# A decoder layer's scan stage: two products for each tile of the small projection, and the attention stage's key stacks loaded by halves of the heads

## The reference

```
x = x + scan(layernorm(x));  x = x + attention(layernorm(x), ctx, ctx);  x = x + experts(layernorm(x))

scan:      xz = x @ W_in.T;  x_proj, z = split(xz)            # 1024 columns each
           x_conv = silu(conv_b + causal convolution over 4 steps)
           x_dbl = x_conv @ W_xproj.T                         # 33 columns: B (16), C (16), dt (1)
           dt = clip(softplus(x_dbl[..., -1]), 0.001, 0.1)
           h = clip(exp(dt*A)*h + clip(dt*B)*x_t, -100, 100);  y_t = h . C
           out = (y*silu(z) + x_conv*D) @ W_out.T
attention: 16 heads of 32; scores = q k^T / sqrt(32); softmax; @ v; @ Wo.T + bo
experts:   top 2 of 8 experts with a capacity; silu(x W1 + b1) W2 + b2
```

## Time and profile before

| | us |
|---|---|
| median of 3 runs | 2587.34 (2586.89 to 2590.86) |
| profiled execution | 2590.91 |
| its span | 2589.3 |
| PE busy in the span | 2419.5 (93%) |
| VectorE busy | 1493.9 (58%) |
| ScalarE busy | 1198.0 (46%) |
| POOL busy | 647.5 (25%) |
| mean granted TensorE clock | 0.968 of full speed |

### The profile page before, as it was taken

How to read it: one execution, slowest core, us unless ns; L and a number is a source line. 1 busy time by engine, 2 the same in 40 slices (tenths; PEclk the granted TensorE clock), 3 DMA queues, 4 the chain that set the end, 5 groups by cost and what they waited for, 6 DMA issues and landing times. The chain is left out here.

```text
span 2589.3 us, 47800 instructions
## 1 busy us (share of the span) xinstructions
PE 2419.5 (93%) x16966; PEld 2129.4 (82%) x16967; DVE 1493.9 (58%) x2584; ACT 1198.0 (46%) x1915; POOL 647.5 (25%) x1040
## 2 busy tenths in 40 slices
PE   7999999999997899999999973599999999999997
PEld 6999999999986788888888852388888888888896
DVE  6778888878873656666666656633343343334322
ACT  6655656656652444444444430234344453434442
POOL 3211211112114445354444411113030321303021
PEclk8999999999998999999999985799999999999998
DMA  4111111111126666656666622234242434424221
GB/s 131 41 40 48 40 38 56 35 43 48 39 73 176 164 183 167 183 163 182 171 180 183 164 74 85 57 117 105 70 124 83 110 82 126 103 72 120 87 53 20
DMA packets 236865, 261.01 MB, mean 101 GB/s; under 512 B 70344, under 2 KB 160456, under 8 KB 236592
## 3 DMA queue, kind: packets, MB, share of 16 engines
q1 hardware_dynamic: 195632, 237.48, 31.3%
q0 software_dynamic: 40960, 20.41, 4.5%
HBM read 182.47 MB, written 68.80 MB: 97 GB/s over the span
## 5 line engine op out<-in xcount | busy, mean ns | idle before, releaser
L2288 DVE TENSOR_TENSOR d_h_l<-d_hf,d_h_h 128x616 fp32r<-128x616 f32 x124 | 99.1, 799 | 392.4 <-ACT d_h_h L2112 392.4
L2017 PE MATMUL d_psH<-d_xgT_h,d_w_l 128*128 128x308 f32 x1024 | 314.5, 307 | 3.0 <-ACT d_hf L2148 2.1
L2018 PE MATMUL d_psH<-d_xgT_l,d_w_h 128*128 128x308 f32 x1024 | 311.5, 304 | 0.0
L2019 PE MATMUL d_psH<-d_xgT_h,d_w_h 128*128 128x308 f32 x1024 | 311.3, 304 | 0.0
L2148 ACT ACTIVATE d_hf<-d_psH,d_b1c 128x308 f32<-128x308 f32 x256 | 130.5, 517 | 383.6 <-PE d_psH L2019 383.5
L439 PE MATMUL a_psP<-s_xnT_h,s_w_l 128*128 128x256 f32 x1024 | 297.5, 291 | 7.2 <-ACT a_zs L691 2.7
L440 PE MATMUL a_psP<-s_xnT_l,s_w_h 128*128 128x256 f32 x1024 | 291.0, 284 | 0.0
L441 PE MATMUL a_psP<-s_xnT_h,s_w_h 128*128 128x256 f32 x1024 | 290.5, 284 | 0.0
L1984 POOL DMA_INDIRECT out_dram<-d_ob,d_to x40 | 103.7, 2592 | 686.0 <-ACT d_ob L2165 676.0
L2017 PE MATMUL d_psO<-d_w_h,d_h_l 128*123 128x512 f32 x620 | 244.2, 394 | 0.0
L2019 PE MATMUL d_psO<-d_w_h,d_h_h 128*123 128x512 f32 x620 | 244.0, 394 | 0.0
(11 more groups left out here) (387 smaller groups left out, 6065.6 us busy)
## 6 DMA issues: line engine op xcount, KB each, us to landing
d_w<-in_W_dram SPq DMA_DIRECT2D x64, 1024.0 KB, 6.2
b_qst<-qs_d SPq DMA_DIRECT2D x48, 512.0 KB, 6.6
b_kst<-ks_d SPq DMA_DIRECT2D x48, 512.0 KB, 6.6
s_raw<-in_x_dram SPq DMA_DIRECT2D x16, 512.0 KB, 3.6
s_xres<-in_x_dram SPq DMA_DIRECT2D x16, 512.0 KB, 3.5
x_d<-s_xres SPq DMA_DIRECT2D x16, 512.0 KB, 2.8
s_raw<-in_ctxT_dram SPq DMA_DIRECT2D x16, 512.0 KB, 9.5
s_xres<-x_d SPq DMA_DIRECT2D x16, 512.0 KB, 10.6
```

What stands on the lines that cost most here:

```text
L2017: pe.matmul(out, lo_w, hi_x, start=first, stop=False)
L2018: pe.matmul(out, hi_w, lo_x, start=False, stop=False)
L2019: return pe.matmul(out, hi_w, hi_x, start=False, stop=last_)
L2288: dve.tensor_tensor(out, a, b_, ALU.subtract).then_inc(done, 1)
```

## The change

- In the scan stage the small projection of a tile is two matmuls instead of three. Of the 128 columns of `wx_h`, those of B and C now stand at 0 to 31 in the high part and at 32 to 63 in the low part, those of dt at 64 to 79 and 96 to 111; `wx_l` holds the rounded weights (columns 0 to 31 and 64 to 79). The first matmul takes `wx_h` and the high data, the second `wx_l` and the low data. Of the bank's rows, two groups have to be added by VectorE: five operations in `rows_1` for three.
- `rows` is now 32 partitions by 513: B and the sums in the first 16 partitions, C in the other 16. `every` is filled by eight DMAs for C, issued once B and C are there, and eight for B and the sums (16 x 513) where all eight were before.
- `xcr_h` and `xcr_l` have four buffers. The small projection follows the in-projection by four tiles; the places of tiles 5, 6 and 7 are as before.
- In the attention stage the key tiles 0 and 1 are stored, SP waits for them to land and loads heads 0 to 7 of the three parts (three DMAs of half the size); then the same for tiles 2 and 3 and heads 8 to 15. PE waits for the first half before its first scores and for the second half before those of the third group of heads.

```diff
+    XB = 4
...
-        xcr_h, xcr_l = sb("xcr_h", [P, 3, S], F32R), sb("xcr_l", [P, 3, S], F32R)
+        xcr_h, xcr_l = sb("xcr_h", [P, XB, S], F32R), sb("xcr_l", [P, XB, S], F32R)
-        rows, every = sb("rows", [N, 3 * S + 1]), sb("every", [P, 3 * S + 1])
-        Bb, Cr, lam = rows[:, 0:S], rows[:, S:2 * S], rows[:, 2 * S:]
+        rows, every = sb("rows", [2 * N, 2 * S + 1]), sb("every", [P, 3 * S + 1])
+        Bb, Cr, lam = rows[0:N, 0:S], rows[N:2 * N, 0:S], rows[0:N, S:]
...
+                    sp.wait_ge(rows_a, 5 * b + 5)
+                    for i in range(NB):
+                        sp.dma_start(every[i * N:(i + 1) * N, 2 * S + 1:], Cr).then_inc(every_ld, 16)
                     sp.wait_ge(rows_b, 12 * b + 5)
                     for i in range(NB):
-                        sp.dma_start(every[i * N:(i + 1) * N, :], rows[:]).then_inc(every_ld, 16)
+                        sp.dma_start(every[i * N:(i + 1) * N, 0:2 * S + 1], rows[0:N, :]).then_inc(every_ld, 16)
...
-                    split_mm(psX[:, 0:S], wx_h[:, i, :], wx_l[:, i, :], xcr_h[:, i % 3, :], xcr_l[:, i % 3, :],
-                             i == 0, i == KE - 1).then_inc(xd_mm, 1)
+                    pe.matmul(psX[:, 0:S], wx_h[:, i, :], xcr_h[:, i % XB, :], start=i == 0, stop=False)
+                    pe.matmul(psX[:, 0:S], wx_l[:, i, :], xcr_l[:, i % XB, :], start=False, stop=i == KE - 1).then_inc(xd_mm, 1)
...
                         in_proj(i, i, x_mm)
-                        if i >= 3:
-                            x_dbl(i - 3)
+                        if i >= XB:
+                            x_dbl(i - XB)
+                    x_dbl(KE - XB)
...
-                        wait(act, xd_mm, 8 * b + i - 2)
-                        copy(xcr_h[:, i % 3, :], xc[par][:, i, :], xc_hi)
+                        wait(act, xd_mm, 8 * b + i - XB + 1)
+                        copy(xcr_h[:, i % XB, :], xc[par][:, i, :], xc_hi)
...
-                        act.wait_ge(rows_a, 3 * b + 3)
+                        act.wait_ge(rows_a, 5 * b + 4)
...
-                cols = [(wx_raw[:, :, 0:N], slice(0, N)), (wx_raw[:, :, N:2 * N], slice(32, 32 + N)),
-                        (wx_raw[:, :, 2 * N:2 * N + 1].broadcast_to([P, KE, N]), slice(64, 64 + N))]
-                for src, at in cols:
-                    ins = dve.tensor_copy(wx_h[:, :, at], src)
+                cols = [(wx_raw[:, :, 0:2 * N], 0, 2 * N),
+                        (wx_raw[:, :, 2 * N:2 * N + 1].broadcast_to([P, KE, N]), 64, N)]
+                for src, at, n in cols:
+                    dve.tensor_copy(wx_l[:, :, at:at + n], src)
+                    ins = dve.tensor_copy(wx_h[:, :, at:at + n], src)
...
-                for src, at in cols:
-                    ins = dve.tensor_tensor(wx_l[:, :, at], src, f32(wx_h[:, :, at]), ALU.subtract)
+                for src, at, n in cols:
+                    ins = dve.tensor_tensor(wx_h[:, :, at + 32:at + 32 + n], src, f32(wx_h[:, :, at:at + n]), ALU.subtract)
...
-                    dve.tensor_scalar(dt_r[:], psX[64:64 + N, 0:S], 5.0, None, ALU.min).then_inc(rows_a, 1)
-                    dve.tensor_copy(Bb, psX[0:N, 0:S]).then_inc(rows_a, 1)
-                    dve.tensor_copy(Cr, psX[32:32 + N, 0:S]).then_inc(rows_a, 1)
+                    dve.tensor_copy(dt_r[:], psX[96:96 + N, 0:S]).then_inc(rows_a, 1)
+                    dve.tensor_copy(rows[:, 0:S], psX[32:64, 0:S]).then_inc(rows_a, 1)
+                    dve.wait_ge(rows_a, 5 * b + 2)
+                    dve.tensor_tensor(dt_r[:], psX[64:64 + N, 0:S], dt_r[:], ALU.add).then_inc(rows_a, 1)
+                    dve.wait_ge(rows_a, 5 * b + 3)
+                    dve.tensor_scalar(dt_r[:], dt_r[:], 5.0, None, ALU.min).then_inc(rows_a, 1)
+                    dve.tensor_tensor(rows[:, 0:S], psX[0:32, 0:S], rows[:, 0:S], ALU.add).then_inc(rows_a, 1)
...
-                    wait(sp, k_ld, 48 * b)
-                    sp.sem_inc(passed_s, 1)
-                    store(ks_d, tk_st, KD)
-                    load(ks_d, tk_st, k_ld, kst[par], (0, 0, 1))
+                    for n in range(2):
+                        wait(sp, k_ld[n], 48 * b)
+                        sp.sem_inc(passed_s, 1)
+                    for n in range(2):
+                        store(ks_d, tk_st, KD, range(2 * n, 2 * n + 2))
+                        load(ks_d, tk_st, k_ld[n], kst[par], (0, 0, 1), 32 * n + 32, slice(n * (H // 2), (n + 1) * (H // 2)))
...
-                            pe.wait_ge(k_ld, 48 * b)
+                            pe.wait_ge(k_ld[0], 48 * b)
...
+                        if j == 2:
+                            pe.wait_ge(k_ld[1], 48 * b)
```

More of the change, by code:

```diff
@@ L729, in _ @@
             dve.memset(ones_row[:], 1.0).then_inc(setup_dve, 1)
-            dve.memset(rows[:, 2 * S:2 * S + 1], 0.0).then_inc(setup_act, 1)
+            dve.memset(rows[0:N, S:S + 1], 0.0).then_inc(setup_act, 1)
             dve.memset(fl[:], 0.0).then_inc(setup_act, 1)
@@ L809, in rows_1 @@
                     wait(dve, rows_d, b)
[L810 removed]
+                    wait(dve, every_ld, 32 * NB * b)
                     wait(dve, m_mm, b)
[L812 to L814 removed]
+                    dve.tensor_copy(dt_r[:], psX[96:96 + N, 0:S]).then_inc(rows_a, 1)
[5 more added lines that the diff above has]
+                    dve.tensor_tensor(rows[:, 0:S], psX[0:32, 0:S], rows[:, 0:S], ALU.add).then_inc(rows_a, 1)
                 def rows_2(part):
@@ L840, in rows_2 @@
                         ch.n = 7
-                        dve.wait_ge(every_ld, 16 * NB * b + 16 * NB)
+                        dve.wait_ge(every_ld, 32 * NB * b + 32 * NB)
                         if first:
                             dve.wait_ge(setup_pool, 11)
-                        sums = every[:, 2 * S:]
+                        sums, C_ = every[:, S:2 * S + 1], every[:, 2 * S + 1:]
                         ch.did(dve.tensor_tensor(refm[:], sums[:, 0:S].rearrange("p (i t) -> p i t", t=BL)[:, :, 0], mine[:, :, 0], ALU.mult))
-                        ch.did(dve.tensor_tensor(every[:, S:2 * S], every[:, S:2 * S], mine[:].rearrange("p i t -> p (i t)"), ALU.mult))
+                        ch.did(dve.tensor_tensor(C_, C_, mine[:].rearrange("p i t -> p (i t)"), ALU.mult))
                         ch.wait()
@@ L855, in rows_3 @@
                     dve.tensor_tensor(EB[:], EB[:], every[:, 0:S], ALU.mult).then_inc(rows_c, 1)
-                    dve.tensor_tensor(EC[:], EC[:], every[:, S:2 * S], ALU.mult).then_inc(rows_c, 1)
+                    dve.tensor_tensor(EC[:], EC[:], every[:, 2 * S + 1:], ALU.mult).then_inc(rows_c, 1)
                 def bounds(part):
@@ L999, in attention_phase @@
         tq_st, tk_st = [sem(f"tq_st{i}") for i in range(2)], [sem(f"tk_st{i}") for i in range(2)]
-        q_ld, k_ld = sem("q_ld"), sem("k_ld")
+        q_ld, k_ld = sem("q_ld"), [sem(f"k_ld{i}") for i in range(2)]
         v_mm, v_cp = sem("v_mm"), sem("v_cp")
@@ L1064, in body, with store @@
             def body(b, par, cur, prev, prev2):
-                def store(scratch, st_, first):
-                    for i in range(KD):
+                def store(scratch, st_, first, tiles):
+                    for i in tiles:
                         sp.wait_ge(qk_lo, U * b + first + i + 1)
@@ L1069, in store, with load @@
                             sp.dma_start(f32(scratch[part, i * P:(i + 1) * P, :]), f32(tile(b, first + i)[part])).then_inc(st_[i % 2], 16)
-                def load(scratch, st_, ld, stack, parts):
+                def load(scratch, st_, ld, stack, parts, stored, heads):
                     for p_ in range(2):
-                        sp.wait_ge(st_[p_], 64 * b + 64)
+                        sp.wait_ge(st_[p_], 64 * b + stored)
                         sp.sem_inc(passed_s, 1)
@@ L1077, in load @@
                     for r, part in enumerate(parts):
-                        sp.dma_start(f32(stack[r * DK:(r + 1) * DK, :, :]),
-                                     f32(scratch[part].rearrange("(h d) s -> d h s", d=DK))).then_inc(ld, 16)
+                        sp.dma_start(f32(stack[r * DK:(r + 1) * DK, heads, :]),
+                                     f32(scratch[part].rearrange("(h d) s -> d h s", d=DK)[:, heads, :])).then_inc(ld, 16)
                 def next_context(b):
@@ L1097, in body @@
                     sp.sem_inc(passed_s, 1)
-                    store(qs_d, tq_st, 0)
-                    load(qs_d, tq_st, q_ld, qst[par], (0, 1, 0))
+                    store(qs_d, tq_st, 0, range(KD))
+                    load(qs_d, tq_st, q_ld, qst[par], (0, 1, 0), 64, slice(0, H))
                 if prev2:
```

4 lines of the change are left out of this document (2 added, 2 removed).

## The result

The changed kernel took 2607.53 us (median of 4 runs, 2601.78 to 2607.80) beside 2589.10 for the kernel before (4 runs, 2586.89 to 2591.41). The ratio is 1.0063, with a 95% interval of 1.0051 to 1.0076. That is 16 us by the ratio (18 between the medians), outside the range that was given (2577 to 2594). The profiled execution took 2607.80, its span is 2606.2.

What follows compares the result with a forecast made beforehand. Each scan batch's end was taken to be set by the chain PE projection, VectorE row reads, ScalarE tables, PE. Scan −2.0, part 3 0 and keys +3.2 gave +1.2 us, 2588.5 from 2587.34; range 2577 to 2594.

Steps and rivals of the forecast that it cites:

- part 4: Attention start, keys by halves: first scores 5.0 us sooner, next stage of that batch later, +3.2 us in all.
- Part 1: Scan stage, two projection products for three: VectorE's row reads start 0.80 us sooner in each batch, bounds 0.5 to 1.2.
- PE's wait before tile 4: Scan stage: PE reaches the projection of tile 4 early and waits 0.65 us for POOL's low part.
- Part 2: Scan stage, VectorE's row reads: five operations for three take 2.0 us, 0.67 more per batch, bounds 0.5 and 0.9.
- Net per batch: Scan stage: reads 0.80 sooner less 0.67 longer, so 0.13 us gained per batch, −2.0 us over 15 batches.
- rival A: Scan stage: PE sets the pace throughout, all its saved work counts, −16 us with part 4, 2571 us; chance 0.10.
- Part 3: Scan stage: the split DMAs for C, the fourth buffer and the last projections cost nothing, 0 us.
- the query tile: Attention start: SP's queue behind the second key half shifts, so the query tile's low part lands 2.0 us later.
- the clock: Attention start: after idling, PE runs the fourth query tile's 12 products at 1.2 GHz, 1.2 us more.
- The sum: Whole kernel: −2.0 + 0 + 3.2 = +1.2 us, median 2588.5 us.

Runs made afterwards that it cites:

- e2: Kernel before with only the new attention stage (keys by halves), scan stage as before: 2595.87 us, ratio 1.0011 to the kernel before.
- e1: Kernel before with only the new scan stage (two-matmul projection), attention stage as before: 2605.27 us, ratio 1.0054 to the kernel before.
- e4: Kernel before plus 160 increments of an unused semaphore in PE's program, not hidden: 2625.12 us, ratio 1.0118 to the kernel before.
- e5: Changed kernel plus 96 semaphore increments on PE, put where PE waits anyway: 2590.76 us, ratio 1.0000 to the kernel before.
- e6: Changed kernel with a third buffer for the low part of query and key tiles: 2586.84 us, ratio 0.9978 to the kernel before.
- e12: Changed kernel plus 256 semaphore increments on PE, one whole packet: 2621.02 us, one run.
- e7: Changed kernel with two row reads for five operations, low-weight columns not added: 2595.17 us, ratio 1.0008 to the kernel before.
- e9: Changed kernel with third buffer, first attention batch's loads between the key halves, minimum folded into the addition: 2582.66 us, ratio 0.9967 to the kernel before.
- e11: Changed kernel plus 48 hidden semaphore increments on PE: 2590.34 us, one run.
- e10: Kernel before with the third buffer alone: 2589.38 us, ratio 0.9993 to the kernel before.
- e3: Changed kernel plus 96 semaphore increments on PE before the attention stage, not all hidden: 2598.45 us, ratio 1.0025 to the kernel before.

## Why the prediction was wrong

- **The step that failed** is the first sentence of part 4, "In steady batches PE doesn't wait for keys", by which the steady attention batches were put at nothing. The sentence is right (e2: 44.95). What was never asked is who else waits in a steady batch, and for what: ScalarE, 46.3 us in 14 batches, at a store. Part 1 reaches it, not part 4. It shortened PE's written-out program by 96 instructions, so the fetch of each 256 fell on that store: +1.05 a steady batch and 14.2 us from the second scores to the last in e1, 12.6 in the changed kernel. e1, e4, e5, e6 and e12 show it, each by another edit.
- **Part 1** held: row reads 0.75 sooner (forecast 0.80); PE's wait before tile 4 was 0.43 (forecast 0.65). Its own terms give the 0.75: tile 7 at 316.4 and the 0.82 from there to the reads less one product make 317.10, not 317.05.
- **Part 2** held: 2.01 (forecast 2.0). Its listed terms add up to 2.02 to 2.13; the 1.90 at which its range begins needs a copy at 0.34. The last addition, back at partition 0 of the bank, started 0.31 after the minimum and the next operation 0.34 after it. The Trainium skill (page "VectorE: DVE Perf Modes", section "Two Vector instructions with no wait between them") had made the sum 2.01 by holding an instruction that starts in another group of 32 partitions; without that rule it was 1.90. The trace agrees with the rule.
- **Net per batch** −0.09 to −0.11, in 15 batches 1.45 us (forecast −0.13 and 2.0). e7 and e9 show that the reads are in the chain, against rival A.
- **Part 3** cost nothing visible.
- **Part 4** held at the start: +2.4 in the changed kernel's one profile, +3.0 between the means of all comparable ones, for +3.2. So did its two terms: 1.6 for the query tile (forecast 2.0), 1.2 for the clock, though 12 products at 0.12 would have made that 1.4. It had nothing for the 1.6 to 1.8 us that the halves win before the last scores.
- **The sum without the failed step** is what e5 measured: 0.0 with ±2.3, beside +1.2, so forecast and no change can't be told apart there. The range had no rival for anything behind the start of the attention stage, and so was too narrow above.
- **Open:** the 5 us behind the last scores. In all fourteen profiles the stretch goes with the granted clock in it: 131.9 to 132.1 us at 0.83 (the kernel before, e2, e5, e11, e12), 134.1 to 135.4 at 0.72 (e1, e4, e10), 136.3 to 137.0 at 0.64 to 0.70 (the others). What sets the clock stays open. It isn't the fetch at 24 us (e12 has it and 0.83, e3 hasn't and 0.64), and no other edit sorts them. Executions of one kernel may well differ in it: one of the changed kernel's four took 2601.78, the others 2607.4 to 2607.8, but only one execution of each kernel was profiled. So of the changed kernel's 16 us the 12.6 are shown by experiments, and the 5 are placed but not explained.

## What to carry to other kernels

In this kernel an edit that changed the number of instructions of an engine whose program is written out also moved its code fetches in everything behind it. Before a saving in one stage is booked, look where a later, periodic stage waits for a DMA with no room to spare, and ask what a packet of 1 us on one engine does there. A third buffer on that wait was the cure that doesn't hang on the place of the fetch (in the kernel before, where none was needed, it brought nothing that can be told); a few idle instructions, hidden in a wait, are the test that tells a moved fetch from the edit itself. And a zero in the sum needs its reason for every engine that waits in the stage, not for PE alone.

## What the hardware did that was not expected

- A fetch of 16 KB of PE's code took 1.0 to 1.1 us of one DMA engine's time, and a 128 KB store that met one landed 1.2 later (4.9 for 3.7).
- The packets come every 256 instructions of PE: 256 more put them back at the same places (24, 34) and the batch back at 46.07; with a body of 768 they stand at the same places in each batch.
- Semaphore increments at PE's start delayed its first matmul by 5.8 us (60 of them), 8.9 (80) and 21.1 (160): 0.10 to 0.13 us each.
- Behind the last scores, with the DMA engines at 0 to 3%, the same work of PE ran at a mean granted clock of 0.64 to 0.83, and took up to 5 us longer for it.
